# Gathering 24 instead of 8 pairs of rows ahead of a graph attention pass, into tiles lent for the time

## The reference, cut to what matters

```python
h = (x @ W.T).reshape(n, h_, d_)
h_src = h[src]
e_src = jnp.einsum('ehd,hd->eh', h_src, a_src)
e_dst = jnp.einsum('ehd,hd->eh', h[dst], a_dst)
e = jax.nn.leaky_relu(e_src + e_dst, NEG_SLOPE)
e = e * (1.0 + et_emb[edge_type])
e = e * edge_weight[:, None]
e_max = jnp.zeros((n, h_), x.dtype).at[dst].max(e)
e = jnp.exp(e - e_max[dst])
e_sum = jnp.zeros((n, h_), x.dtype).at[dst].add(e)
alpha = e / (e_sum[dst] + 1e-10)
msg = h_src * alpha[:, :, None]
out = jnp.zeros((n, h_, d_), x.dtype).at[dst].add(msg).reshape(n, h_ * d_)
```

## Time and profile before

| what | value |
|---|---|
| median of three runs | 1938.15 us (1935.38 to 1944.36) |
| profiled execution | span 1934.6 us, from its first to its last instruction; its time outside the span isn't listed apart |
| mean granted clock of TensorE | 0.929 of full speed |
| busy in the span: PE, DVE, POOL, ACT | 1608.4, 1167.7, 705.2, 471.2 us |
| DMA | 248.96 MB, mean 129 GB/s |
| `edge_scores` | from about 949 to 1089 us |
| `attention_weights` | from about 1090 to 1134 us |
| `attention_pass` | from about 1135 to 1356 us |

### The profile page before, as it was taken

One profiled execution on the slowest core, in us unless ns is written; L12 is line 12 of the kernel. 1 busy time (PEld: TensorE's weight loads), 2 busy tenths in 40 slices (PEclk: granted clock), 3 DMA queues, 4 the chain that ended last, 5 costly groups with the idle time before them and its releaser, 6 DMA issues. The chain is left out here.

```text
span 1934.6 us, 27686 instructions
## 1 busy us (share of the span) xinstructions
PE 1608.4 (83%) x7565; PEld 981.3 (51%) x7566; DVE 1167.7 (60%) x2310; ACT 471.2 (24%) x884; POOL 705.2 (36%) x605
## 2 busy tenths in 40 slices
PE   6755956776498999998888459998498899999998
PEld 6751633335443555554555435554246545874486
DVE  5779958884365777775467766665774832113222
ACT  4301103432212555554344210000110111001100
POOL 0001877887094776660000347775330010000000
PEclk9997988998698999999899569999799999999999
DMA  0017844005802766682388337776104201430033
GB/s 25 0 47 285 275 136 120 1 1 172 306 27 92 210 197 187 187 169 45 126 317 331 101 100 211 210 209 171 27 1 144 96 1 72 155 122 1 0 136 135
DMA packets 76346, 248.96 MB, mean 129 GB/s; under 512 B 14901, under 2 KB 28582, under 8 KB 68346
## 3 DMA queue, kind: packets, MB, share of 16 engines
q1 hardware_dynamic: 38618, 147.08, 21.1%
q0 software_dynamic: 34592, 96.87, 18.9%
q10 hardware_dynamic: 3072, 4.20, 0.7%
HBM read 215.93 MB, written 32.00 MB: 128 GB/s over the span
## 5 line engine op out<-in xcount | busy, mean ns | idle before, releaser
L664 POOL DMA_INDIRECT tab_slots<-slot_words,slot_address x160 | 238.1, 1488 | 244.5 <-issue 233.3
L693 POOL DMA_INDIRECT e_rows<-tab_h,idx_h x176 | 178.6, 1015 | 293.4 <-POOLq L50 219.8
L1443 PE MATMUL dense_pY<-weights,dense_xT_block 128*128 128x512 f32 x640 | 284.3, 602 | 0.0
L1491 PE MATMUL dense_pY<-parts,dense_number 128*128 128x512 f32 x1000 | 237.7, 399 | 7.1 <-DMA dense_number<-tab_edges_to 7.1
L994 POOL DMA_INDIRECT e_rows<-tab_q,idx_q x192 | 182.0, 948 | 99.4 <-issue 38.9
L1491 PEld LDWEIGHTS dense_pY<-parts,dense_number 128*128 128x128 f32 x1000 | 188.7, 189 | 54.8 <-DMA dense_number<-tab_edges_to 8.6
L787 PE MATMUL e_pS<-e_rows,e_onehot_ring 128*128 128x512 f32 x352 | 194.2, 643 | 22.1 <-DVE e_rows L763 19.2
L1443 PEld LDWEIGHTS dense_pY<-weights,dense_xT_block 128*128 128x128 f32 x640 | 121.9, 194 | 143.1 <-issue 143.1
L1067 PE MATMUL e_pS<-e_rows,e_onehot_f 128*128 128x512 f32 x384 | 181.4, 596 | 0.0
L877 PE MATMUL count_pA<-count_onehot_d,count_onehot_s 128*128 128x512 f16 (+1 forms) x576 | 117.4, 352 | 63.8 <-DVE count_onehot_d L855 60.3
L763 DVE TENSOR_TENSOR e_rows<-e_rows,e_pW 128x1024 f32<-128x1024 f32 x88 | 107.3, 1220 | 69.3 <-DMA e_rows<-tab_h,idx_h 69.0
(11 more groups left out here) (312 smaller groups left out, 2448.4 us busy)
## 6 DMA issues: line engine op xcount, KB each, us to landing
basis_piece<-in_L_gnn_basis_pieces SPq DMA_DIRECT2D x32, 2048.0 KB, 7.9
dense_number<-tab_edges_from SPq DMA_DIRECT2D x20, 1280.0 KB, 5.4
tab_edges_from<-counts_turned SPq DMA_DIRECT2D x10, 1280.0 KB
tab_edges_to<-counts_total SPq DMA_DIRECT2D x10, 640.0 KB
dense_number<-tab_edges_to SPq DMA_DIRECT2D x10, 640.0 KB, 4.6
tab_w<-basis_wout ACTq DMA_DIRECT2D x128, 32.0 KB
weights<-tab_w SPq DMA_DIRECT2D x4, 1024.0 KB, 6.3
weights<-in_L_gnn_W_T SPq DMA_DIRECT2D x3, 1024.0 KB
```

The source lines that it names most:

```text
L664: pool.indirect_dma_start(self.table, bass.IndirectOffsetOnAxis(self.address[:, t:t + 1], 0), self.words[:, t, :], None).then_inc(self.pla ...
L693: pool.indirect_dma_start(self.rows[:, q, s, :], None, self.table, bass.IndirectOffsetOnAxis(self.idx[:, j * 2 + s:j * 2 + s + 1], 0)).the ...
L1443: ins = self.nc.tensor.matmul(self.banks.at(g), self.xt[:, b % 2, c, :], weights[:, c, :], start=c == 0, stop=c == 3)
L1491: ins = self.nc.tensor.matmul(self.banks.at(self.first + b), self.number[:, b % 2, r * NB + k, :], self.parts[r][n][:, k, :], start=k == 0 ...
```

## The change

The ring keeps its 8 places and gets 16 more for the first 16 pairs. Of these 15 are lent by tiles that hold nothing in that time: 5 by `acc` (the sums), 6 by the three weight tiles (2 each), 4 by the eight vectors; one is new. Each of the 16 has a semaphore of its own.

- The 16 pairs (32 indirect DMAs) are gathered by POOL in `edge_scores`.
- In `attention_weights` POOL gathers 8 pairs as before, now pairs 16 to 23. The two weight loads are gone from there.
- In `attention_pass` POOL begins with pair 24, which needs pair 16 to be summed (the wait's formula is the same). It issues 128 indirect DMAs instead of 160. DVE and PE run two steps unrolled instead of one, with the rows in the lent places. ACT waits for five pairs before it writes `acc` for the first time. SP, which had nothing there, waits for `summed` of 17, which is the end of pair 15, and then loads the two weight matrices (1 MB each) and the seven vectors (256 KB each as written to 128 partitions).
- In the load stage the seven vectors are no longer loaded.

```diff
+FIRST_STEPS = 2
+FIRST = FIRST_STEPS * BODYP
...
-        self.rows = ctx.enter_context(nc.sbuf_tensor(f"{name}_rows", [P, BODYP, 2, D], F32))
+        self.ring = ctx.enter_context(nc.sbuf_tensor(f"{name}_rows", [P, BODYP, 2, D], F32))
+        own = FIRST - len(lent)
+        more = ctx.enter_context(nc.sbuf_tensor(f"{name}_first_rows", [P, own, 2, D], F32))
+        self.first = lent + [more[:, k, :, :] for k in range(own)]
         self.got = [sem(f"got{q}") for q in range(BODYP)]
+        self.got_first = [sem(f"got_first{j}") for j in range(FIRST)]
+
+    def rows(self, i, u):
+        if isinstance(i, int) and i < FIRST_STEPS:
+            return self.first[i * BODYP + u]
+        return self.ring[:, u, :, :]
+
+    def wait_rows(self, eng, i, u):
+        if isinstance(i, int) and i < FIRST_STEPS:
+            eng.wait_ge(self.got_first[i * BODYP + u], 32)
+        else:
+            eng.wait_ge(self.got[u], (i + (1 - FIRST_STEPS)) * 32)
...
         @block.gpsimd
         def _(pool):
-            for j in range(BODYP, PAIRS):
+            for j in range(FIRST + BODYP, PAIRS):
                 pool.wait_ge(summed, j + 2 - BODYP)
                 ring.gather(pool, j)
+
+        @block.sync
+        def _(sp):
+            sp.wait_ge(summed, 1 + FIRST)
+            for tile, source in loads:
+                sp.dma_start(tile, source).then_inc(loaded, 16)
+            for tile, source, arrived in vectors:
+                sp.dma_start(tile, source).then_inc(arrived, 16)
+            sp.wait_ge(loaded, 16 * len(loads))
...
+            act.wait_ge(summed, 1 + lent_back)
...
-            lagged(v, NSTEP, BODYP, [(0, build), (0, multiply)])
+            peeled(v, NSTEP, step, first=FIRST_STEPS)
...
-            peeled(pe, NSTEP, step)
+            peeled(pe, NSTEP, step, first=FIRST_STEPS)
...
@@ edge_scores
+        @block.gpsimd
+        def _(pool):
+            for j in range(FIRST):
+                ring.gather(pool, j)
...
@@ attention_weights
-        @block.sync
-        def _(sp):
-            for tile, source in weights:
-                sp.dma_start(tile, source).then_inc(weights_in, 16)
-            sp.wait_ge(weights_in, 16 * len(weights))
...
         @block.gpsimd
         def _(pool):
-            for j in range(BODYP):
+            for j in range(FIRST, FIRST + BODYP):
                 ring.gather(pool, j)
...
@@ gnn
-                for k in range(1, len(VECS)):
-                    sp.dma_start(vec[:, k, :], ins[VECS[k]].partition_broadcast(P)).then_inc(vecs_in, 16)
...
+        pairs_of = lambda tile, n: [tile[:, 2 * k:2 * k + 2, :] for k in range(n // 2)]
+        ring = RowRing(nc, until_dense, "e1", tab["h"], idx["h"],
+                       pairs_of(acc, NB) + sum((pairs_of(w, 4) for w in W), []) + pairs_of(vec, len(VECS)))
```

More of the change, by code:

```diff
@@ L704, in attention_pass @@
         sem = stage_semaphores(nc, ctx, name)
-        rows, got = ring.rows, ring.got
         ohr = sb("onehot_ring", [P, 4, 2, P], F32)
@@ L712, in attention_pass @@
         summed, taken, emptied = sem("summed"), sem("taken"), sem("emptied")
+        loaded = sem("loaded")
         block = ctx.enter_context(nc.Block())
@@ L760, in multiply @@
             def multiply(i, u):
-                v.wait_ge(got[u], (i + 1) * 32)
-                r = rows[:, u, :, :].rearrange("p s (h d) -> p s h d", h=H)
+                ring.wait_rows(v, i, u)
+                r = ring.rows(i, u).rearrange("p s (h d) -> p s h d", h=H)
                 nc.vector.tensor_tensor(
@@ L765, in multiply, with step @@
                     ALU.mult).then_inc(weighted, 1)
-            lagged(v, NSTEP, BODYP, [(0, build), (0, multiply)])
+            def step(i):
+                for u in range(BODYP):
+                    build(i, u)
+                    multiply(i, u)
+            peeled(v, NSTEP, step, first=FIRST_STEPS)
         @block.tensor
@@ L786, in step @@
                     for s in range(2):
-                        nc.tensor.matmul(flat(pS[:, bass.ds(bank[u], 1), :]), ohr[:, u % 4, s, :], rows[:, u, s, :],
+                        nc.tensor.matmul(flat(pS[:, bass.ds(bank[u], 1), :]), ohr[:, u % 4, s, :], ring.rows(i, u)[:, s, :],
                                          start=False, stop=True, skip_group_check=True)
@@ L1753, in edge_scores @@
 def edge_scores(nc, name, C, identb, est, edt, src_lo, src_block, loc, pair_block, es_out, ed_out,
-                basis):
+                basis, ring):
     U = 4
@@ L1907, with attention_weights @@
 L = SLOTS // PAIRS * P
-def attention_weights(nc, name, C, es, ed, factor, loc, block_f, wt, weights, ring):
+def attention_weights(nc, name, C, es, ed, factor, loc, block_f, wt, ring):
     with ExitStack() as ctx:
@@ L1937, in attention_weights @@
         sem = stage_semaphores(nc, ctx, name)
-        weights_in = sem("weights_in")
         s_dve, scored_ready, laid, seq_out, first_out = (
```

24 lines of the change are left out of this document (12 added, 12 removed).

## The result

| | before | after |
|---|---|---|
| median of ten runs each | 1938.07 us (1933.25 to 1944.36) | 1947.28 us (1944.01 to 1952.42) |
| profiled execution, and its span | 1934.6 us span | 1947.18 us, span 1945.4 us |
| mean granted clock of TensorE | 0.929 | 0.921 |
| busy: PE, DVE, POOL | 1608.4, 1167.7, 705.2 us | 1614.1, 1165.4, 706.0 us |

The ratio is 1.0052, with a 95% interval of 1.0039 to 1.0065: the change makes the kernel slower by half a per cent. The forecast was 1938.8 us in a range of 1932.0 to 1950.0, with "within 0.5%" as the likeliest case. The range holds the time; the result lies on the upper edge of that case (the two medians are 9.2 us apart, just inside the edge of 9.7, and the ratio of 1.0052 is just outside it). The sum is off by 8.5 us: it said nearly no change, and it is the width of the range, not the sum, that caught the result.

What follows compares the result with a forecast made beforehand. POOL's gathers were taken to bound the pass, and PE's pieces, with hardly any DMA slack, `edge_scores`. -5.4 + 6 = +0.6 us on the 1934.6 span gave 1935.2; with the median 3.55 above the span, 1938.8 us, range 1932.0 to 1950.0.

Steps and rivals of the forecast that it cites:

- within 0.5%: Whole kernel: the time differs from the kernel before by less than 0.5% (9.7 us); chance 0.76.
- The pass, -5.4 us: Attention pass: POOL has 128 gathers left and starts its last at 1336.8 instead of 1342.15, -5.4 us.
- The 32 gathers in `edge_scores`, +6 us: `edge_scores`: the gathers take DMA time from the pieces, so the last piece comes later, +6 us.
- rival 2: `edge_scores`: pieces come 13.7 us late and PE's clock falls, 7 us more; +15.3 in all, 1953.4 us; chance 0.20.
- Both ends, 0 and 14: `edge_scores`: bounds on the gathers' delay, 0 if pieces are served first, 14 us at 0.93 us a gather.
- Rival 1: `edge_scores`: the gathers are hidden and the pieces keep their pace, only the pass's 5.4 us count; 1932.8 us; chance 0.22.
- Rival 3: Pass: the 3.9 MB of loads meet POOL's start, POOL waits for places, 4 of 5.4 us lost; 1942.8; chance 0.10.
- The softmax, the load stage, the unrolled steps and ACT's wait, 0 each: Softmax, load stage and pass: moved weight and vector loads, unrolled steps and ACT's wait for five pairs cost 0 each.
- DVE beside POOL, 0: `edge_scores`: the gathers slow DVE by at most 5 us, hidden under its own waits; counted 0, 5 kept for the range.
- The 5 us, and the 10 for equal halves: `edge_scores`: the gathers' cost is about +5 us if queues alternate packet by packet, +10 if they share in equal halves.
- The signs named: Profile after: last portion about 1070, wrong if unchanged or past 1078; PE's single waits 3 us or more; DVE waits 55 us.

Runs made afterwards that it cites:

- ring24: Changed kernel with all 24 places reused, 10 pairs gathered after the pieces, 8 in the softmax, all 11 steps unrolled; 1916.88 us, ratio 0.9897 to before.
- beside24: Kernel before with 24 gathers added in `edge_scores` from its start, into idle tiles, rows used by nobody; 1944.23 us, ratio 1.0024 to before.
- late12: Changed kernel with no gathers beside the pieces: 12 pairs after piece 15 of 16 landed, 12 in the softmax; 1949.93 us, ratio 1.0062 to before.
- late10: Changed kernel with 10 pairs gathered after the pieces, 8 in the softmax, pairs 18 to 23 at the pass's start; 1941.86 us, again 1941.95.

## Why the prediction was right and where it failed

**The pass, -5.4 us: right.** 5.2 us in the profiled pair of traces, 6.2 in the repeated one (217.2 and 211.0). The steps hold too: POOL's first gather 35.0 us after pair 0 (34.9 said), the last one 193.8 (193.6), DVE's waits 55.1 us (55). The reason given for its being only a quarter of what is there, that the ring's own 8 places are full while PE eats the first 16 pairs, is what ring24 bears out from the other side: with a like head start (18 pairs against 24), but the lent places used again, PE hardly waits (192.63 us busy of 196) and 23.6 us come; "20 us before today's last multiply" was the right size.

**The 32 gathers in `edge_scores`, +6 us: the step that failed.** The term held only the DMA time that the gathers take. That part was well sized: their queue took 21.6 us of all engines, where 21 to 30 were said, and 6.8 us were lost while they ran (8.1 and 9.2 against the mean of six traces; beside24 makes it 6.7). The stage lost 13.1 us (15.9 in the repeated pair). What the term left out is the other 6.3 us, lost after the last gather had landed: the pieces land after 8.5 us instead of 7.8, each step of four portions waits 0.9 us for a piece, two portions from there on run slower, and a step takes 13.6 us instead of 12.3, nearly five steps long. I had the slack of 0.6 us and PE's clock on the page and put them into rival 2, as something that decides only beyond 15 us. Both ends, 0 and 14, were right as ends, and the value between them was chosen from the nearer DMA row without asking what a late piece does to the pieces after it.

What made those 6.3 us is not shown. Being late isn't enough: the kernel before waits 1.06 us for a piece and beside24 2.2 us, and both are back at 12.3 us a step. Gathers aren't needed: late12 and late10 have the slow rhythm without them. So the sum failed by a term that was put at nothing, its size is measured, and its cause stays open.

**Rival 2** was right in its sign and nearest in what it describes, late pieces and slower matmuls behind them. Its 7 us for the slower PE are near the 6.3, though more than half of these are waits; its 13.7 for the gathers is about twice what came, and so is the whole too large: 9.2 us against 15.3. **Rival 1** fell: the stage grew, and the DMA share of 1.01 at 400 GB/s left nothing to hide in while the gathers ran. **Rival 3** fell: POOL had no wait for a place behind the new loads. It issued at 1.25 us throughout, and the longest DVE wait beside the 3.9 MB was 1.62 us:

```profile
1209.82 1.22 DVE L792 TENSOR_TENSOR e_rows<-e_rows,e_pW 128x1024 f32<-128x1024 f32 x1 [1.62 <-DMA e_rows<-tab_h,idx_h]
```

The gathers issued in 1186 to 1230 landed after 5.1 us in the middle, near the 5.4 of the earlier trace rows, and after 3.7 later on. **The softmax, the load stage, the unrolled steps and ACT's wait, 0 each**: 48.5 against 48.6 us in the softmax, and 1.15 us in all ahead of `edge_scores`, which is within what the kernel before does from trace to trace (949.3 and 951.1). **DVE beside POOL, 0**: DVE's busy time is 1165.4 instead of 1167.7 us, and from 970 to 1000, beside the gathers, one of its instructions took 18.37 / 48 = 0.38 us where it took 20.59 / 55 = 0.37. The other direction, DVE's scans holding up POOL's issues in the softmax (late12), the prediction didn't have; 16 gathers fitted there all the same.

**The pages of the skill.** By "DMA: Bandwidth & Descriptors" (Queues, rings and completion order) of the Trainium skill, queues take turns packet by packet, from which I drew gathers that stretch over the stage and a cost of about 5 us. The trace agrees in part: from 950 to 1012 the pieces' queue had 59.9% of the engines' time and the gathers' 34.9%, and the last gathers landed after 19.7 us. But the gathers were through in 61 us and not stretched over the stage, and a piece was not shielded, 10.3 us instead of 7.9. The 5 us, and the 10 for equal halves, weren't worked out from anything; 6.8 came. The 358 GB/s of "HBM Reference" (Specifications) of the Trainium skill is given there as a core's share when both cores of a pair stream, and the section says that a core alone gets more; the prediction tried it as a ceiling. This trace agrees with the section: 400 GB/s over 30 us.

**The signs named.** The last portion came at 1078.03 us, where "about 1070" was said and "later than 1078" was to count as wrong: by its own line the step was wrong, here by a hair, and clearly in the repeated trace (1081.29). The single waits of 2.9 us (3 or more said) just miss, the DMA share of 0.92 to 1.01 was as said, and the gathers were issued by 993.6 and landed by about 1012 (1010 said). DVE first waits for a gather at 1209.82, 35.2 us later than before (35 said).

## What to carry to other kernels

A deeper head start pays little if the places are not used again at once (5.2 us here, 23.6 with reuse): price the idle time of the engine that fills them before pricing the pairs in hand. Look for the slack of each double-buffered load before laying new traffic beside it, and look at the trace behind the new traffic too: here about half of the loss came after it, and in late12 and late10, which took the traffic away, that half stayed. And a stage ends with its last issue: work moved into a short stage because its engine idles there (24 gathers in the softmax) can hold the barrier, the more so if its issues take longer there than elsewhere.

## What the runs showed of the hardware

- Two rhythms of the same loop of 2 MB loads: issues 6.1 to 6.3 us apart, landing after 7.7 to 8.0 us, 12.3 us a step at a DMA share of 0.95 (before, 1015 to 1055); or uneven issues, most often 5.8 and some 7.8 us apart by turns, landing after 8.5 to 8.7 (8.0 to 10.1 in late10's two traces), 13.3 to 13.8 us a step in the mean at 0.84 to 0.90, also with no other traffic beside the pieces (late10, late12).
- Indirect gathers of 128 rows of 2 KB beside loads of 2 MB landed after 9.7 us at first and 19.7 at last instead of 3.7; together they ran at 400 GB/s over 30 us, where the loads alone had 363 over 55 us.
- POOL issues such gathers at 1.25 us each beside a busy PE and DVE in the pass; in ring24 that was 208 GB/s over 196 us with PE busy 98%, with one wait of 3.9 us for a place. In the softmax an issue beside a 4.42 us scan of DVE took 4.05 to 4.59 us instead of 0.95.
- The last pairs of the kernel before run slower than POOL, 3.6 us apart, at a DMA share of 0.80 and only 151 GB/s:

```profile
1336.00:1351.00 15.00, 10.07 (x36) 5.44 (x35) 6.20 (x8) 0.00 (x0) 5.57 (x6) 1.00 0.80 151
```

That the slots there hold no edges and all name the same row, and that this makes them slow, is likely; the one was not read out, the other not tried.
